# Compressed interaction network on one core: four banks multiplied and added field by field on VectorE, six scaled on ScalarE

## The reference

```python
Xi = X0
for W, b in Ws:                                   # W: (128, 39 * Fi)
    Wr = W.reshape(H, F0_, Fi)
    Xi = jnp.einsum('hjk,bjd,bkd->bhd', Wr, X0, Xi) + b[None, :, None]
    res.append(Xi.sum(axis=2))
z = jnp.concatenate(res, axis=1)
h = jnp.maximum(jnp.concatenate([z, dense_ctx], 1) @ W_top1 + b_top1, 0.0)
h = jnp.maximum(h @ W_top2 + b_top2, 0.0)
y = h @ W_top3
```

## Time and profile before

| what | value |
|---|---|
| median of 3 runs | 657.25 us (656.97 to 657.32) |
| the profiled execution, its span from the first to the last instruction | 664.5 us; the page gives no other time of it |
| granted TensorE clock | 0.995 of full speed over the span |
| busy share PE / DVE / ACT / POOL | 95% / 85% / 84% / 67% |
| first layer-1 tile starts at | 45.7 us |
| one group, groups 3 to 14 | 35.1 to 35.2 us each |
| after the last layer-1 matmul | 613.7 to 664.5 us |

### The profile page before, as it was taken

One profiled execution on the slowest core, in us unless ns is written; L12 is line 12 of the kernel. 1 busy time (PEld: TensorE's weight loads), 2 busy tenths in 40 slices (PEclk: granted clock), 3 DMA queues, 4 the chain that ended last, 5 costly groups with the idle time before them and its releaser, 6 DMA issues.

```text
span 664.5 us, 11375 instructions
## 1 busy us (share of the span) xinstructions
PE 633.7 (95%) x2616; PEld 477.0 (72%) x2616; DVE 561.9 (85%) x878; ACT 557.3 (84%) x1940; POOL 443.1 (67%) x504
## 2 busy tenths in 40 slices
PE   2689999999999999999999999999999999989998
PEld 2656767777777777777777777777777777767874
DVE  3538788889899898989898989898989989899890
ACT  2348788989898999999998999998989998999773
POOL 7555897777777778687777787777777535152700
PEclk9799999999999999999999999999999999999999
DMA  8245533242424233242423333323242320200000
GB/s 292 22 61 105 162 38 87 51 87 56 84 56 80 59 58 84 40 102 33 90 41 84 57 86 55 87 52 81 57 85 55 67 68 6 69 27 0 1 0 1
DMA packets 91117, 43.58 MB, mean 66 GB/s; under 512 B 80630, under 2 KB 83780, under 8 KB 88943
## 3 DMA queue, kind: packets, MB, share of 16 engines
q1 hardware_dynamic: 84058, 41.77, 28.1%
q0 software_dynamic: 5120, 1.29, 2.2%
q10 hardware_dynamic: 1904, 0.15, 0.2%
HBM read 36.39 MB, written 1.81 MB: 57 GB/s over the span
## 4 chain that ended last, share of the span: by engine, by line
PE 75%; DVE 8%; ACT 7%; issue 6%; DMA 3%; DVEq 1%; POOL 0%; SPq 0%; another core or an unknown queue 0%
PE yb L1128 16%; PE yb L1124 16%; PE yb L1125 16%; PE p L1089 10%; PE pq L1101 6%; ACT yb L765 5%; DVE x L941 3%; DVE acc L935 3%; DMA gram<-in_L_rec_W_dram 2%; PE yb L1026 2%; DMA emb<-in_table_dram,idx 1%; DVE x1l L896 1%; PE yb L1237 1%; PE p L1182 1%; PE p L1214 1%
## 5 line engine op out<-in xcount | busy, mean ns | idle before, releaser
L765 ACT ACTIVATE yb<-yb,x0t 128x128 f32<-128x128 f32 x1728 | 467.2, 391 | 56.0 <-PE yb L1128 49.6
L935 DVE TENSOR_TENSOR acc<-acc,yb 128x512 f32<-128x512 f32 (+1 forms) x512 | 323.4, 674 | 33.8 <-ACT yb L765 30.9
L1124 PE MATMUL yb<-w1h,x1h 128*128 128x512 f32 (+1 forms) x640 | 293.8, 459 | 5.0 <-DVE acc L935 3.8
L1128 PE MATMUL yb<-w1h,x1l 128*128 128x512 f32 (+1 forms) x640 | 247.4, 387 | 0.0
L1125 PE MATMUL yb<-w1l,x1h 128*128 128x512 f32 (+1 forms) x640 | 247.1, 386 | 0.0
L497 POOL DMA_INDIRECT emb<-in_table_dram,idx x160 | 153.0, 956 | 53.1 <-issue 44.4
L1124 PEld LDWEIGHTS yb<-w1h,x1h 128*128 128x128 f32 x640 | 120.1, 188 | 59.4 <-DVE acc L935 25.3
L1125 PEld LDWEIGHTS yb<-w1l,x1h 128*128 128x128 f32 x640 | 120.5, 188 | 39.6 <-issue 18.0
L1128 PEld LDWEIGHTS yb<-w1h,x1l 128*128 128x128 f32 x640 | 120.1, 188 | 24.8 <-DVE x1l L896 0.4
L568 POOL TENSOR_TENSOR late<-late,x0r 117x512 f32<-117x512 f32 (+1 forms) x105 | 132.7, 1298 | 4.6 <-DMA late<-x_scratch 4.3
L544 POOL TENSOR_TENSOR bdiag<-mask,x0t 128x312 f32<-128x312 f32 x64 | 45.7, 714 | 107.0 <-PE pq L1101 106.4
(11 more groups left out here) (124 smaller groups left out, 377.2 us busy)
## 6 DMA issues: line engine op xcount, KB each, us to landing
late<-x_scratch SPq DMA_DIRECT2D x45, 312.0 KB
late<-x_scratch SPq DMA_DIRECT2D x30, 234.0 KB
x0r<-x_scratch SPq DMA_DIRECT2D x15, 234.0 KB
emb<-in_table_dram,idx POOLq DMA_INDIRECT x160
gram<-in_L_rec_W_dram SPq DMA_DIRECT2D x1, 2496.0 KB
late<-x_scratch SPq DMA_DIRECT2D x15, 156.0 KB
spare<-spare SPq DMA_DIRECT2D x28, 78.0 KB
x_scratch<-emb SPq DMA_DIRECT2D x75, 20.0 KB
```

The costliest lines, as they stand in the source:

```text
L765: op = act.activation(part, part, ACT.Copy, scale=x0t[u][:, t, j:j + 1])
L935: dve.tensor_tensor(part, part, parts(y_bank(t, m), n), ALU.add).then_inc(summed, 1)
L1124: pe.matmul(y[:, 0:w], hi, w1h[:, at:at + w], start=True, stop=False)
L1128: pe.matmul(y[:, 0:w], lo, w1h[:, at:at + w], start=False, stop=True).then_inc(bank_ready, 1)
```

## The change

DVE multiplies and adds banks 0, 3, 6 and now 9 field by field: one SCALAR_TENSOR_TENSOR of 128 columns per field, `acc_part = field * x + acc_part`, into two partial sums in turn (the first starts from the bias `b1c`, the second with a TENSOR_SCALAR). ACT scales six banks (24 fields in place of 27) and writes the first of them, bank 1, into `acc` itself, where DVE used to start the sums. DVE adds the other five (2, 4, 5, 7, 8). The accumulator is laid out [part, output] instead of [output, part] and has six parts instead of nine, so that the fold reads every 128th number. `SEAM_ORDER` is gone: the fold has the same place in all tiles. The bias copies of ACT (L817) are gone. DVE's loop over groups becomes a written-out program.

```diff
-ACT_BANKS = (1, 2, 4, 5, 7, 8, 9)
-DVE_BANKS = (0, 3, 6)
+ACT_BANKS = (1, 2, 4, 5, 7, 8)
+DVE_BANKS = (0, 3, 6, 9)
...
+FIRST_BANK = ACT_BANKS[0]
+FUSED_AT = BANK_F
+N_FUSED_PARTS = 2
+PARTS = BANK_F + N_FUSED_PARTS
+DVE_ORDER = (("sum before", 8), ("fuse before", 9), ("fuse", 0), ("fold before", 0), ("fuse", 3), ("sum", 2),
+             ("sum", 4), ("fuse", 6), ("sum", 5), ("sum", 7))
+SUM_ORDER = (2, 4, 5, 7, 8)
...
-        acc = [sb(f"acc{u}", [P, HID, PARTS]) for u in range(2)]
+        acc = [sb(f"acc{u}", [P, PARTS, HID]) for u in range(2)]
...
-                        sp.wait_ge(dve_scaled, g * (TILES * N_DVE))
+                        sp.wait_ge(fused, g * (TILES * N_FUSED))
...
                 act.wait_ge(bank_ready, T * BANKS + m + 1)
+                if m == FIRST_BANK and at_least(T, 2):
+                    act.wait_ge(x2_ready, T - 1)
...
-                    op = act.activation(part, part, ACT.Copy, scale=x0t[u][:, t, j:j + 1])
+                    dst = acc[t % 2][:, i, :] if m == FIRST_BANK else part
+                    op = act.activation(dst, part, ACT.Copy, scale=x0t[u][:, t, j:j + 1])
...
-            def scale(g, t, u, m):
+            def fuse(g, t, u, m):
...
                 y = y_bank(t, m)
...
+                for i in range(fields_of(m)):
+                    j = BANK_F * m + i
+                    k = fused_before(m) + i
+                    part = acc[t % 2][:, FUSED_AT + k % N_FUSED_PARTS, :]
+                    field, x = y[:, i * HID:(i + 1) * HID], x0t[u][:, t, j:j + 1]
+                    if k == 0:
+                        dve.scalar_tensor_tensor(out=part, in0=field, scalar=x, in1=b1c[:, :],
+                                                 op0=ALU.mult, op1=ALU.add).then_inc(fused, 1)
+                    elif k < N_FUSED_PARTS:
+                        dve.tensor_scalar(part, field, x, None, ALU.mult).then_inc(fused, 1)
+                    else:
+                        dve.wait_ge(fused, T * N_FUSED + k - N_FUSED_PARTS + 1)
+                        dve.scalar_tensor_tensor(out=part, in0=field, scalar=x, in1=part,
+                                                 op0=ALU.mult, op1=ALU.add).then_inc(fused, 1)
...
             def add_bank(T, t, m):
...
+                part = acc[t % 2][:, 0:n, :]
+                dve.tensor_tensor(part, part, y_bank(t, m)[:, 0:n * HID].rearrange("p (j h) -> p j h", h=HID),
+                                  ALU.add).then_inc(summed, 1)
...
             def fold(T, t):
...
-                dve.tensor_reduce(x2[t % 2][:, :], acc[t % 2][:, :, :], AX.X, ALU.add).then_inc(x2_ready, 1)
+                dve.tensor_reduce(x2[t % 2][:, :], acc[t % 2][:, :, :].rearrange("p j h -> p h j"), AX.X,
+                                  ALU.add).then_inc(x2_ready, 1)
...
-            with dve.Fori(1, GROUPS // 2 - 1) as it:
+            for it in range(1, GROUPS // 2 - 1):
...
             def bank_free(T, m):
...
-                if m in BEGINS:
-                    pe.wait_ge(dve_scaled, T * N_DVE + BEGINS.index(m) + 1)
+                if m in DVE_BANKS:
+                    pe.wait_ge(fused, T * N_FUSED + fused_before(m) + fields_of(m))
+                elif m == FIRST_BANK:
+                    pe.wait_ge(act_scaled, T * N_ACT + 1)
                 else:
                     pe.wait_ge(summed, sums_by(T, m))
```

More of the change, by code:

```diff
@@ L257, in tower @@
         act_scaled = sem("act_scaled")
-        dve_scaled = sem("dve_scaled")
+        fused = sem("fused")
         summed = sem("summed")
@@ L299, in sums_by, with fused_before @@
             return T * N_SUM + SUM_ORDER.index(m) + 1
+        N_FUSED = sum(fields_of(m) for m in DVE_BANKS)
+        def fused_before(m):
+            return sum(fields_of(k) for k in DVE_BANKS if k < m)
         ACT_SPLIT = tuple(c for c in SPLIT if c in ACT_HIGH)
@@ L814, in _ @@
             act.activation(b2s[:, :], b2c[:, :], ACT.Copy, scale=float(DIM)).then_inc(bias_ready, 1)
-            act.wait_ge(b1_in, 16)
-            for u in range(2):
-                act.activation(acc[u][:, :, PARTS - 1], b1c[:, :], ACT.Copy).then_inc(bias_ready, 1)
             high_part(0, 0)
@@ L898, in low_part @@
                                          op1=ALU.subtract).then_inc(x1l_ready, 1)
-            def parts(y, n):
-                return y[:, 0:n * HID].rearrange("p (j h) -> p h j", h=HID)
-            def scale(g, t, u, m):
+            def fuse(g, t, u, m):
                 T = g * TILES + t
@@ L908, in scale @@
                 dve.wait_ge(bank_ready, T * BANKS + m + 1)
+                if m == DVE_BANKS[0] and at_least(T, 2):
+                    dve.wait_ge(x2_ready, T - 1)
                 y = y_bank(t, m)
-                if m in BEGINS:
[L911 to L917, removed]
@@ L918, in scale @@
-                y = y[:, :].rearrange("p (j h) -> p j h", h=HID)
-                dve.tensor_tensor(y, y, x0t[u][:, t, BANK_F * m:BANK_F * (m + 1), None].to_broadcast([P, BANK_F, HID]),
-                                  ALU.mult).then_inc(dve_scaled, 1)
+                for i in range(fields_of(m)):
[12 more added lines that the diff above has]
+                                                 op0=ALU.mult, op1=ALU.add).then_inc(fused, 1)
@@ L922, in add_bank @@
             def add_bank(T, t, m):
                 n = fields_of(m)
[L924 to L932, removed]
@@ L933, in add_bank @@
-                at = BANK_F * (k % N_ACC)
-                part = acc[t % 2][:, :, at:at + n]
-                dve.tensor_tensor(part, part, parts(y_bank(t, m), n), ALU.add).then_inc(summed, 1)
+                if m != SUM_ORDER[0]:
+                    dve.wait_ge(summed, sums_by(T, m) - 1)
+                dve.wait_ge(act_scaled, T * N_ACT + ACT_BANKS.index(m) + 1)
+                part = acc[t % 2][:, 0:n, :]
+                dve.tensor_tensor(part, part, y_bank(t, m)[:, 0:n * HID].rearrange("p (j h) -> p j h", h=HID),
+                                  ALU.add).then_inc(summed, 1)
@@ L937, in fold @@
             def fold(T, t):
                 dve.wait_ge(summed, (T + 1) * N_SUM)
+                dve.wait_ge(fused, (T + 1) * N_FUSED)
                 if at_least(T, 2):
                     dve.wait_ge(gram_done, T - 1)
-                dve.tensor_reduce(x2[t % 2][:, :], acc[t % 2][:, :, :], AX.X, ALU.add).then_inc(x2_ready, 1)
+                dve.tensor_reduce(x2[t % 2][:, :], acc[t % 2][:, :, :].rearrange("p j h -> p h j"), AX.X,
+                                  ALU.add).then_inc(x2_ready, 1)
@@ L945, in period @@
                     T = g * TILES + t
-                    for kind, m in SEAM_ORDER if t == TILES - 1 and more else DVE_ORDER:
-                        if kind == "scale":
-                            scale(g, t, u, m)
+                    for kind, m in DVE_ORDER:
+                        if kind == "fuse":
+                            fuse(g, t, u, m)
                         elif kind == "sum":
@@ L953, in period @@
                                 add_bank(T - 1, (t + TILES - 1) % TILES, m)
+                            elif kind == "fuse before":
+                                fuse(g if t > 0 else g - 1, (t + TILES - 1) % TILES, u if t > 0 else 1 - u, m)
                             else:
@@ L972, in _ @@
             low_part(0, 0)
-            dve.wait_ge(bias_ready, 3)
+            dve.wait_ge(bias_ready, 1)
+            dve.wait_ge(b1_in, 16)
             period(0, 0, True)
             period(1, 1, True)
-            with dve.Fori(1, GROUPS // 2 - 1) as it:
+            for it in range(1, GROUPS // 2 - 1):
                 period(it * 2, 0, True)
@@ L983, in _ @@
                     add_bank(NT - 1, TILES - 1, m)
+                elif kind == "fuse before":
+                    fuse(GROUPS - 1, TILES - 1, 1, m)
             fold(NT - 1, TILES - 1)
```

## The result

The changed kernel took 680.32 us (679.68 to 680.55, 4 runs) against 657.11 us (656.95 to 657.32, 4 runs) of the kernel before beside it: ratio 1.035, 95% interval 1.0338 to 1.0363, so 23.2 us slower. The forecast was 671.7 us with a range of 657 to 692: the direction, the place and the mechanism came out, of the amount 14.4 of 23.2 us.

A forecast was written before the change was run, and what follows sets the result against it. The prediction took PE, busy 95% of the span, as the bound, with stalls where groups begin. Its terms 12.4 + 1 + 1 = +14.4 us on 657.25 gave 671.7 us, range 657 to 692.

The forecast's parts named there:

- Bank 3 behind bank 9 behind bank 8: PE's bank 3 waits for DVE's bank 9, behind bank 8's sum: stalls of 2.10 us per group replace 1.07.
- The fields: DVE's fused multiplications of 128 columns: 347 ns each, the next starting after 0.26 us, 3.9 us per tile.
- become the bound: Rival: DVE's fields step above 0.296 us, so groups last as long as DVE works; 683 us and up, chance 0.20.
- The fold: DVE's reduction of 768 numbers, each 512 bytes from the last: 1.55 us, lower end 0.95.
- ACT's bank 8: At the change of group ACT has bank 8 ready at 334.94, unmoved by the change.
- The sums stay at 0.59 us: DVE's five plain sums per tile keep their step of 0.59 us, 2.97 us per tile.
- Groups 0 to 2: ACT, the late one there, gains 3 us, but the same wait appears: +1 us.
- The last group: DVE's either way: 33.4 us without the low part against 32.8, +1 us.
- Written out: I take 0: DVE's program written out instead of looped costs 0 us, bounds -1 and +3.
- The carry-over from span to median: Profiled span lies 7.25 us above the median; this difference was carried over, from 678.9 to 671.7 us.
- The sum by stretch: Layer 1's stretches: twelve regular groups +12.4 us, groups 0 to 2 +1, last group +1, together +14.4.
- The faster rival: Bank 9 is drained before PE comes to bank 3, so the stalls vanish: 642 us, half of it 650; chance 0.12.

The follow-up runs named there:

- the chain undone: Changed kernel with the sums of banks 4 and 7 sent to a second buffer, so no sum waits for the one just before: 674.37 us, ratio 1.0274.
- B2: The kernel before, unchanged, profiled a second time: span 655.6 us, layer 1 beginning at 40.21 us.

## Why the prediction was right, and where it fell short

- **Bank 3 behind bank 9 behind bank 8:** right. Moving bank 9 ahead gives back 23.7 us. The loads wait where it was said, and the gram product doesn't: 0.58 us in the third tile (0.50 predicted), 0.23 in the fourth (0.15), and 0.85 for bank 0 and 0.87 for bank 3 where a group begins (1.45 together).
- **The fields:** predicted 347 ns and a step of 0.26 us; measured 341 and 258 to 260 ns. DVE did not become the bound: in a regular group it is busy 34.9 of 36.7 us.
- **The fold:** predicted 1.55 us, measured 1.51; "at full rate 0.95", measured 0.94. The two rows of sums over far-apart numbers were a good guide. The Trainium skill's 1.73 ns a column for one source that hops at every element (Vector Engine (DVE) Microarchitecture Reference, "Measured stream behaviour on trn2") gave an estimate of 1.48, and the trace agrees.
- **ACT's bank 8:** predicted 4.12 us after the high part starts (330.82 to 334.94), measured 4.09 (332.07 to 336.16): right.
- **"The sums stay at 0.59 us": this is the step that failed.** A sum directly behind a sum steps 0.72 us (0.68, then 0.03), since each waits for the end of the one before; the 0.59 of the earlier trace rows was read where two accumulators take turns, and the change leaves one. Between the low part and bank 8's sum stand two such steps, one more stands right ahead of the low part, and DVE starts bank 8's sum 0.44 us after ACT has the bank ready, where the text said 0.03 and "DVE idle before that sum". Its own numbers put DVE there at 332.11 + 0.66 + 1.03 + 2 x 0.59 = 334.98 against ACT's 334.94: a tie that I didn't work out, and any longer step decides it. The stalls became 2.59 in place of 2.10 us per group. Where DVE isn't late, with the chain undone or the fold read in a row, bank 3's load comes 5.71 and 5.73 us after ACT's high part starts; the prediction has 5.66 (330.82 to 336.48), the changed kernel 6.05. So the path was right, and DVE's arrival on it was put too early.
- **Groups 0 to 2:** +1 predicted, +2.4 measured. The relief of ACT that the text counted on there wasn't to be had: group 0 gained nothing (36.30 against 36.31), and in B2 it is PE that fills group 1 (busy 37.38 of 37.78 us), not ACT (34.09). The last group: +1 predicted, +1.2 measured.
- **"Written out: I take 0":** the kernel before loses about 1 us by it, inside the bounds given. That the changed kernel needs it (27.9 us) was not seen.
- **The carry-over from span to median** was wrong: the profiled execution of before had a preparation 5.5 us longer than B2, and groups 0 to 2 took 2.3 longer (111.54 against 109.25). The forecast span (678.9) comes near the measured 677.9 only because this error and the short stall cancel, by luck. The forecast of 671.7 us itself adds 14.4 to the median and doesn't hang on it.
- **The sum by stretch:** groups 3 to 14 took 19.5 us more in place of the predicted 12.4. With the chain undone they take 436.08 us in place of 440.56, so it makes 4.5 of the 7.1 us between; writing out may make 1 more, which was measured on the kernel before alone. The rest, some 1.6 us, is not told apart.
- **The faster rival** came true in the version with bank 9 first and the fold's numbers side by side: 5.2 us, not 15, as bank 0 and bank 3 keep waiting behind the low part.

## What to carry to other kernels

When a buffer moves to another engine, follow its release in that engine's order: here one entry that reads a bank PE needs soon stood behind one that waits for a third engine, and 3.5% hung on their order. When two things arrive at one point, work out both arrivals; the one not named as the releaser is late as soon as a step grows. And don't carry the distance between one profiled execution and the median over to another kernel before a second profile shows that it belongs to the kernel.

## What the runs showed of the hardware that was not expected

- DVE's additions with both inputs in SBUF: 128 columns took 291 to 294 ns with no TENSOR_TENSOR of POOL beside them, 1446 ns in the mean and up to 3.69 us beside one.
- A DVE loop pass of 408 instructions lost 2.73 to 2.99 us at each jump back, one of 270 only 0.12 to 0.16. After each of these jumps PE had stood waiting (4.35 us at the one shown), and TensorE's granted clock was then 0.50 for 3.41 us, once for 6.83.
- In these runs single numbers far apart cost time in SBUF and not in PSUM. In SBUF it was 0.74 ns more per number that DVE read (fold), (443 - 343)/128 = 0.78 per number it wrote, and (489 - 369)/128 = 0.94 per number ACT wrote; the sums that read PSUM 512 bytes apart took 686 ns, those that read it in a row 683.
- A DVE instruction that waits for the one before it starts 34 ns after its end, 123 ns where the waited value is in a register (in the loop); without such a wait it starts 80 to 90 ns before that end.
